# Low parts of a third of the up weights by an accumulating transfer, and the second tile's last third of the up projection in high and low parts

## What is computed

```python
y = mask * (conv(mask * x, K) + D * mask * x)       # [64*64, 1024]
scores = y @ Wr.T                                   # 64 experts, the best 16 kept, softmax
h = einsum('nd,krd->nkr', y, A)                     # up: 1024 -> 64 experts x rank 16
out = x + 2 * einsum('nkr,kdr->nd', h * gates, B)   # down: 1024 -> 1024
```

## Time and profile before

| | |
|---|---|
| median of 3 runs | 894.25 us (894.18 to 894.29) |
| profiled execution | 894.25 us |
| its span, first to last instruction | 892.5 us |
| TensorE matmuls busy | 879.5 us (99%) |
| VectorE busy | 753.8 us (84%) |
| ScalarE busy | 376.1 us (42%) |
| GpSimd busy | 6.5 us (1%) |
| granted TensorE clock | 1.00 in the whole span |
| DMA | 103.32 MB, 116 GB/s on the mean |

### The profile page before, as it was taken

How to read it: one execution, slowest core, us unless ns; L and a number is a source line. 1 busy time by engine, 2 the same in 40 slices (tenths; PEclk the granted TensorE clock), 3 DMA queues, 4 the chain that set the end, 5 groups by cost and what they waited for, 6 DMA issues and landing times.

```text
span 892.5 us, 15771 instructions
## 1 busy us (share of the span) xinstructions
PE 879.5 (99%) x4478; PEld 781.4 (88%) x4478; DVE 753.8 (84%) x2597; ACT 376.1 (42%) x642; POOL 6.5 (1%) x22
## 2 busy tenths in 40 slices
PE   5999999999999999999999999999999999999998
PEld 3667999998889998889999889999889999889997
DVE  8989998988889888889888889888889888888722
ACT  5763563444444344444344444334444334442100
POOL 2000000000000000000000000000000000000000
PEclk9999999999999999999999999999999999999999
DMA  7721315444333444333444434444333445333331
GB/s 238 241 57 47 77 33 141 141 118 121 115 120 108 124 118 126 115 119 111 118 118 131 113 117 110 118 118 137 110 116 108 118 118 141 111 114 114 93 95 48
DMA packets 74759, 103.32 MB, mean 116 GB/s; under 512 B 23972, under 2 KB 56804, under 8 KB 74740
## 3 DMA queue, kind: packets, MB, share of 16 engines
q1 hardware_dynamic: 74212, 102.63, 40.2%
q0 software_dynamic: 160, 0.10, 0.2%
q10 hardware_dynamic: 368, 0.36, 0.1%
HBM read 67.34 MB, written 34.93 MB: 115 GB/s over the span
## 4 chain that ended last, share of the span: by engine, by line
PE 95%; DVE 3%; ACT 1%; issue 0%; DMA 0%; ACTq 0%; DVEq 0%
PE out_ps L1432 26%; PE h_ps L1432 19%; PE out_ps L1436 13%; PE h_ps L1436 9%; PE turn_ps L1432 8%; PE turn_ps L1436 4%; PE conv_ps L1388 2%; PE conv_ps L1389 2%; PE conv_ps L1390 2%; PE conv_ps L1361 1%; PE conv_ps L1398 1%; PE conv_ps L1362 1%; PE conv_ps L1399 1%; PE conv_ps L1400 1%; PE conv_ps L1363 1%; PE h_ps L1441 1%
## 5 line engine op out<-in xcount | busy, mean ns | idle before, releaser
L1432 PE MATMUL out_ps<-b_lo,g_hi 128*128 128x512 f32 x496 | 196.1, 395 | 0.0
L1432 PE MATMUL out_ps<-b_hi,g_hi 128*128 128x512 f32 x496 | 194.7, 393 | 0.3 <-ACT g_hi L584 0.3
L1432 PE MATMUL h_ps<-a_hi,y_hi 128*128 128x384 f32 x480 | 161.4, 336 | 0.0
L1432 PE MATMUL h_ps<-a_lo,y_hi 128*128 128x384 f32 x480 | 161.3, 336 | 0.0
L1436 PE MATMUL out_ps<-b_hi,g_lo 128*128 128x512 f32 x496 | 122.6, 389 | 0.0
L1432 PEld LDWEIGHTS out_ps<-b_lo,g_hi 128*128 128x128 f32 x496 | 93.2, 188 | 21.2
L1432 PEld LDWEIGHTS out_ps<-b_hi,g_hi 128*128 128x128 f32 x496 | 93.0, 188 | 20.4 <-ACT g_hi L584 0.9
L1436 PEld LDWEIGHTS out_ps<-b_hi,g_lo 128*128 128x128 f32 x496 | 93.0, 188 | 20.0
L857 DVE SCALAR_TENSOR_TENSOR z<-swapped,step_other,part 128x64 f32<-128x64 f32 x384 | 92.3, 282 | 11.9
L850 DVE SCALAR_TENSOR_TENSOR part<-z,step_own,conv_ps 128x64 f32<-128x64 f32 x384 | 90.5, 277 | 8.7 <-ACT z L486 0.4
L1436 PE MATMUL h_ps<-a_hi,y_lo 128*128 128x384 f32 x480 | 93.1, 336 | 0.0
(11 more groups left out here) (244 smaller groups left out, 1480.7 us busy)
## 6 DMA issues: line engine op xcount, KB each, us to landing
xt_in<-in_xt SPq DMA_DIRECT2D x32, 512.0 KB, 3.3
x_in<-in_x SPq DMA_DIRECT2D x62, 256.0 KB, 3.7
out<-x_in SPq DMA_DIRECT2D x62, 256.0 KB, 3.1
moved<-square_sb SPq DMA_DIRECT2D x28, 512.0 KB, 2.7
square_sb<-moved SPq DMA_DIRECT2D x112, 128.0 KB, 2.9
b_in<-in_b_t SPq DMA_DIRECT2D x8, 512.0 KB, 7.8
a_in<-in_a_t SPq DMA_DIRECT2D x8, 512.0 KB, 9.1
moved_in<-square_in SPq DMA_DIRECT2D x26, 128.0 KB, 2.8
```

The source lines that it names most:

```text
L1432: pe.matmul(o, hi[:, c, :], moving[:, c, columns], start=first and c == order[0] and moving is w_hi, stop=False)
```

## The change

For columns 0 to 384 (the third part) `a_lo` is no longer made by VectorE. ScalarE first writes the high parts of those columns for chunks 4 to 7 (`high_last`), and then writes the negative of the weights, rounded to fp32r, over the weights themselves (`minus_high`). GpSimd then issues one transfer that reads the weights from HBM again and adds them onto what lies there: minus the high part plus the weight is the low part. Both ScalarE instructions stand behind `decays(2)`. The splits at the end of `first_step` leave out the columns that are done already (`split_rest`).

With this low part there early, tile 1's third part of the up projection uses the split form, for which ScalarE makes `y_hi` of tile 1 (`high_y(1, i)`, behind `first_copies(2)`) and VectorE `y_lo` (`low_y(1, i)`, behind `gate(1)`). VectorE's `low_up(2)` is gone, and `low_up(0)` and `low_up(1)` move to the places of `low_up(1)` and `low_up(2)`.

```diff
@@ gpsimd, at the end of its program
+            pool.wait_ge(s_minus_hi, 1)
+            pool.dma_start(a_lo[:, :, 0:384], a_t[:, :, 0:384], accum_op=ALU.add).then_inc(s_alo[2], 16)
@@ scalar
+            def high_last():
+                for i in LATE[5:]:
+                    act.wait_ge(s_w[i], 16)
+                act.activation(a_hi[:, NC // 2:NC, 0:384], a_in[:, NC // 2:NC, 0:384], ACT.Copy).then_inc(s_hilast, 1)
+            def split_rest(i):
+                _, arrived, hi, _ = loads[i]
+                act.activation(hi[:, 384:ER], arrived[:, 384:ER], ACT.Copy).then_inc(s_whi, 1)
+            def minus_high(n, up_before, highs):
+                _, c0, width, _ = H_PARTS[n]
+                act.wait_ge(s_up, up_before)
+                act.wait_ge(s_hilast, 1)
+                act.wait_ge(s_whi, highs)
+                act.activation(a_lo[:, :, c0:c0 + width], a_in[:, :, c0:c0 + width], ACT.Copy, scale=-1.0).then_inc(s_minus_hi, 1)
@@ scalar, first_step
                 decays(2)
+                high_last()
+                minus_high(2, 3, len(HIGH) - 4)
                 sines(2)
...
                 first_copies(2)
+                for i in range(HT):
+                    high_y(1, i)
                 tables(3)
                 for i in LATE[5:]:
-                    split_weights(i)
+                    split_rest(i)
@@ vector, second_step
                 gate(1)
+                for i in range(HT):
+                    low_y(1, i)
                 states(2, range(MIDDLE, FED))
                 gates_of(1)
                 gate_part(1, 0)
-                low_up(0)
                 low_near(2)
...
                 low_in(3)
-                low_up(1)
+                low_up(0)
                 for i in range(HT):
                     low_y(2, i)
                 low_x(3)
-                low_up(2)
+                low_up(1)
@@ tensor, up
-                    if first:
+                    if first and n < 2:
                         pe.wait_ge(s_wlo, len(MIDST) + n + 1)
@@ tensor, second_step
-                for n in range(len(H_PARTS)):
+                for n in range(2):
                     for c in range(NC):
                         last = whole_product(n, c)
                     last.then_inc(s_up, 1)
+                o, c0, width, _ = H_PARTS[2]
+                pe.wait_ge(s_yhi, HT)
+                pe.wait_ge(s_alo[2], 16)
+                product_high(o, y_hi, a_hi, a_lo, slice(c0, c0 + width), range(NC), first=True)
+                pe.wait_ge(s_ylo, HT)
+                product_low(o, y_lo, a_hi, slice(c0, c0 + width), range(NC)).then_inc(s_up, 1)
```

More of the change, by code:

```diff
@@ L207, in build @@
         s_whi, s_wlo = sem("s_whi"), sem("s_wlo")
+        s_hilast, s_minus_hi, s_alo = sem("s_hilast"), sem("s_minus_hi"), [sem(f"s_alo_{n}") for n in range(3)]
         s_theta, s_whole, s_args, s_sine, s_decay, s_powers, s_other, s_raw = (
@@ L878, in low_y @@
                 head = slice(i * B, (i + 1) * B)
-                dve.wait_ge(s_yhi, HT * (t - EXACT) + i + 1)
+                dve.wait_ge(s_yhi, HT * (t + 1 - EXACT) + i + 1)
                 dve.tensor_tensor(out=y_lo[:, :, head], in0=y_m[:, :, head], in1=y_hi[:, :, head].bitcast(F32),
@@ L1451, in up @@
                     if n == 0:
-                        pe.wait_ge(s_ylo, HT * (t - EXACT) + HT)
+                        pe.wait_ge(s_ylo, HT * (t + 1 - EXACT) + HT)
                     product_low(o, y_lo, a_hi, slice(c0, c0 + width), range(NC)).then_inc(s_up, 1)
@@ L1549, in third_step @@
                 pe.wait_ge(s_glo, 4)
-                pe.wait_ge(s_yhi, HT)
+                pe.wait_ge(s_yhi, 2 * HT)
                 up(2, True, first=True)
@@ L1567, in step @@
                 pe.wait_ge(s_hg, 3 * t)
-                pe.wait_ge(s_yhi, HT * (t - EXACT) + HT)
+                pe.wait_ge(s_yhi, HT * (t + 1 - EXACT) + HT)
                 up(t, conv)
```

## The result

The changed kernel takes 899.98 us (median of 6 runs, 899.36 to 900.55) against 894.2 us before (median of 6, 893.94 to 894.29), a ratio of 1.0065 with a 95% interval of 1.0052 to 1.0078: slower by 5.8 us. Forecast were 894.3 us and a range of 893.0 to 898.0. The profiled execution took 900.55 us, with a span of 898.8.

What follows compares the result with a forecast made beforehand. TensorE was taken to bound the kernel. From 894.25 us, -1.00 for the third part, +1.03 for the later `load_x(2)` and 0 for VectorE, ScalarE and the transfer's own landing gave 894.3 us, range 893.0 to 898.0.

Steps and rivals of the forecast that it cites:

- What bounds the kernel: Whole kernel: TensorE, whose chain ended last for 95% of the span, waiting only 0.4 and 0.2 us from 42 us on.
- a stall ahead of `feed(2)`: TensorE before tile 2's feed: any new wait is lost in full, since nothing later would absorb it.
- The gain on TensorE: Tile 1's third part of the up projection: 5.16 us falls to 4.16 in the split form, 1.00 us gained.
- ScalarE: Two new copies behind `decays(2)`: 1.47 and 2.72 us, fitting the idle time before `sines(2)` with 0.9 us to spare, no cost.
- VectorE: Loses `low_up(2)` (3.35 us), gets `low_y(1)` (1.29 us), moves two others: no bound here, costed at nothing.
- The place of the collision and the slack: The transfer meets `load_x(2)`, issued at 51.83 and landing at 55.13, with 0.15 us of slack before TensorE's `feed(2)`.
- The transfer itself: Accumulating rows of 147 ns, 64 on each engine: 9.4 us, done at 62 to 64, no wait at the third part.
- The issue: GpSimd issuing the accumulating transfer of 1024 rows, from about 49.5: about 2.8 us.
- The step that failed: At `load_x(2)`: engines alternate rows, each of 8 load rows waits for one of 147 ns, 1.18 us.
- Rival (b): `load_x(2)` goes behind the transfer's queued rows: stall 3.4 us, time 896.6, up to 899.0; over 2.8 us of stall, chance 0.11.
- The rule of the Trainium skill: At `load_x(2)`: engines alternate queues by packets of 9 to 17 descriptors; stall 1.2 to 2.4 us, 894.4 to 895.6 us.
- 1.03 us forecast for the stall: TensorE ahead of `feed(2)`: 1.18 us of delay to `load_x(2)` less 0.15 us of slack.

Runs made afterwards that it cites:

- e1: The changed kernel without its accumulating transfer, TensorE waiting for `minus_high` in place of the landing: 893.71 us, ratio 0.9989 to the kernel before.
- e8: The changed kernel itself, unaltered, run again on the same chip as three other runs: 901.00 us, ratio 1.0069 to the kernel before.
- e5: The changed kernel with the same transfer as a plain write instead of an accumulating one: 900.25 us, ratio 1.0058 to the kernel before.
- e10: The changed kernel with a plain transfer of the same bytes issued from ScalarE's queue behind `minus_high`, not by GpSimd: 898.88 us, ratio 1.0052 to the kernel before.
- e7: The changed kernel with the accumulating transfer issued as eight transfers, one for each chunk: 898.14 us, ratio 1.0039 to the kernel before.
- e6: The changed kernel with the transfer cut to the first two of the eight chunks: 895.12 us, ratio 1.0004 to the kernel before.
- e3: The changed kernel with 17 matmuls of 128 x 128, their result unread, put ahead of `feed(2)`: 898.29 us, ratio 1.0044 to the kernel before.
- e9: The changed kernel with the transfer waiting for the same event that releases `load_x(2)`: 893.65 us, ratio 0.9991 to the kernel before.
- e11: The changed kernel with the transfer released together with `load_x(2)` and tile 1's third part taking its `a_lo` products last: 893.62 us, ratio 0.9991 to the kernel before.
- e2: The changed kernel with GpSimd waiting for the landing of `load_x(2)` before issuing the transfer: 895.68 us, ratio 1.0017 to the kernel before.

## Why the prediction was wrong

**Right.** What bounds the kernel, and that a stall ahead of `feed(2)` is lost in full: the end moved by 6.30 us, the turning by 6.26. The gain on TensorE: 1.01 us measured, 1.00 forecast. ScalarE: 1.50 and 2.77 us for the two copies, against 1.47 and 2.72, inside the idle time. VectorE: no wait on it, e1 shows the new order to be free. The place of the collision and the slack: the load was 4.1 us later (7.4 against 3.3), TensorE's stall 4.01 longer. The transfer itself: 464 rows from 59.7 to 63.2 at a share of 1.16 are 3.5 x 1.16 x 16 / 464 = 140 ns each, where 147 were worked out, and it landed at 64.2, forecast 62 to 64, without a wait on it. The issue took 1.75 us, not 2.8.

**The step that failed** is "If the engines take a row of one and a row of the other in turn, each of the 8 rows waits for one of 147 ns: 1.18 us". The turns are there once the load has begun, and at about this price: in the trace's records of single rows, two rows of the load start most often 150 ns apart in e1, where it is alone, and 280 to 290 ns apart in the profile after, with a row of the transfer starting as nearly each row of the load ends. That is 8 x 0.13 to 0.14 us, 1.1 us. What I had wrong is when the load begins: with the transfer issued 1.7 to 2.4 us ahead of it, the load's first row comes 3.3 (after), 4.0 (e8), 4.1 (e5) and 4.0 us (e10) after its issue, not 1.0. That puts 2.3 to 3.1 us ahead of what I had priced. The remaining 0.7 us in the profile after and 0.8 in e8 (4.1 and 4.9 us late in all) would fit engines that don't all begin the load at once: between its first and its last row 276 rows of the transfer start in the profile after and 207 in e8, where turns on all engines from the first row on would make 128. Rival (b), with 0.11, came nearest: it had the wait behind what is queued, but priced it as several rows for each of the load's own, which the turns don't show.

The rule of the Trainium skill that I put beside it (DMA: Bandwidth & Descriptors, section Queues, rings and completion order) has whole packets, typically 9 to 17 descriptors and 64 at most. Counting a row as a descriptor, the rows that go ahead of the load's first are 149 in the profile after (9 for each of the 16 engines), 158 in e7 (10), 231 in e6 (14), 375 in e8 (23), 667 in e5 (42) and 833 in e10 (52): three of six are beyond the typical figure, none beyond the most. But once both are running they change over row by row, and not after a packet of that size. So the rule points the right way for the head wait, and its typical figure holds neither there in general nor for the turns.

**The second thing, which the prediction left out altogether**, is the clock. I priced a stall at its own length. After 3.2 us of nothing to do TensorE's clock fell to half, and that added 2.78 us in the profile after: 1.03 us forecast for the stall turned into 6.8. e3 separates the two, as a stall of about the same length without the fall. With the measured stall alone the sum would have been 894.25 + 4.01 - 1.01 = 897.3, inside the range; in that profile the clock took it out. That isn't so in every run: e3, with the load 0.7 us later still and without the fall, took 898.29, a little above the range.

**What stays open** is what the load waits for at the head. The number of rows that pass it differs widely (9 to 52 for each engine), the time less (3.3 to 4.1 us from its issue with a whole transfer ahead, 2.3 with a quarter, 1.7 with eight pieces), and it is there without the addition (e5) and from another queue (e10). It isn't needed that rows of the transfer move before the load is issued: in the profile after the first of them starts at 53.06, 0.8 us behind the load's issue and 0.2 us before the load alone would have begun. In e9 and e11 the wait is gone, but there the transfer begins only when the load is through. No run has the load first and both on the engines, so whether the order or the overlap decides isn't shown.

## What to carry to other kernels

A large transfer that is released a little ahead of a small one on which the critical path waits can cost far more than its share of the engines. Here it was enough to tie it to the event that releases the small one (e8 against e9: 7 us between two kernels that differ in one wait), since its own rows start only 2.2 us after its issue, when the small one is through. Before costing a new transfer, look in the trace for loads whose landing has no slack, and assume that they can wait at the head, not only share. And a stall on a TensorE-bound path has a second price above some length: here one of 1.9 us (e2) left the clock alone and one of 3.4 us (e7) did not, so a forecast needs both sums.

## What the runs showed of the hardware that was not expected

A load of 512 KB issued 1.7 to 2.4 us behind 1.57 MB on another queue had no row on the 16 engines for 3.3 to 4.1 us from its issue (1.0 alone), with the transfer accumulating or plain, by GpSimd's queue or ScalarE's. After that the two queues took turns row by row. An accumulating row of 1536 B took 140 ns, a plain one about 87 ns at its best (216 rows from 55 to 56 us at a share of 1.172 in e5), a ratio of 1.6, both into an fp32r tile. TensorE's granted clock fell to 0.50 at 3.2 us into the idle stretch of the profile after, between 2.3 us (e7) and 3.5 us (e10) in the others, and in the profile after it stayed there through the first 5.8 us of matmuls that followed; 34 short records in the gap kept it at 1.0.
